# A gated graph network on one core: gates before the state update, row sums one chunk earlier, the residual kept in DRAM

## The reference, cut to what matters

```python
state = x
for _ in range(5):
    s_in, s_out = state @ in_W.T + in_b, state @ out_W.T + out_b
    a_in, a_out = A @ s_in, A.T @ s_out
    a = concat([a_in, a_out, state])
    r, z = sigmoid(a @ r_W.T + r_b), sigmoid(a @ z_W.T + z_b)
    joined = concat([a_in, a_out, r * state])
    h_hat = tanh(joined @ h_W.T + h_b)
    state = (1 - z) * state + z * h_hat
out = tanh(state @ o1_W.T + o1_b) @ o2_W.T + o2_b
return layernorm(x + out)
```

## Time and profile before

| | before |
|---|---|
| median of 3 runs | 700.49 us |
| profiled execution, its own time | 700.8 us |
| its span (first to last instruction) | 699.0 us |
| PE busy | 665.0 us, 2940 matmuls |
| DVE busy | 528.2 us |
| ACT busy | 348.8 us |
| POOL busy | 61.9 us |
| granted TensorE clock, mean | 0.986 |

### The profile page before, as it was taken

How to read it: one execution, slowest core, us unless ns; L and a number is a source line. 1 busy time by engine, 2 the same in 40 slices (tenths; PEclk the granted TensorE clock), 3 DMA queues, 4 the chain that set the end, 5 groups by cost and what they waited for, 6 DMA issues and landing times.

```text
span 699.0 us, 8537 instructions
## 1 busy us (share of the span) xinstructions
PE 665.0 (95%) x2940; PEld 539.7 (77%) x2940; DVE 528.2 (76%) x838; ACT 348.8 (50%) x486; POOL 61.9 (9%) x56
## 2 busy tenths in 40 slices
PE   8999999979999998999999989999998999999894
PEld 8888888757887886788778767877886788787783
DVE  4976776899577858867686797687768957856886
ACT  2955463646256236625452664356074715623555
POOL 0040204910000000000000000000000000004302
PEclk9999999989999999999999999999999999999998
DMA  9991621221000221200003021000312100013003
GB/s 294 379 371 45 229 67 49 42 61 30 3 0 31 57 35 43 35 13 0 30 33 57 15 46 30 0 30 30 51 40 60 30 1 1 8 61 120 1 1 123
DMA packets 91474, 44.62 MB, mean 64 GB/s; under 512 B 72112, under 2 KB 80944, under 8 KB 91184
## 3 DMA queue, kind: packets, MB, share of 16 engines
q1 hardware_dynamic: 87088, 43.67, 22.0%
q10 hardware_dynamic: 4352, 0.53, 0.5%
HBM read 32.12 MB, written 9.44 MB: 59 GB/s over the span
## 4 chain that ended last, share of the span: by engine, by line
PE 70%; DVE 16%; ACT 8%; issue 4%; ACTq 0%; POOL 0%; DVEq 0%; POOLq 0%
PE bank L546 25%; PE bank L597 12%; PE bank L533 10%; PE bank L535 10%; PE bank L534 10%; DVE work L1226 3%; ACT ring L792 2%; ACT ring L814 2%; DVE work L1245 2%; ACT work L885 2%; DVE work L1248 2%; DVE rows L1094 2%; PE bank L690 2%; DVE work L1232 1%; DVE stateT L1253 1%
## 5 line engine op out<-in xcount | busy, mean ns | idle before, releaser
L546 PE MATMUL bank<-ring,rows 128*128 128x512 f32 x768 | 178.6, 389 | 0.0
L885 ACT ACTIVATE work<-work,bias 128x512 f32<-128x512 f32 x120 | 85.8, 722 | 180.1 <-DVE work L1226 179.9
L546 PEld LDWEIGHTS bank<-ring,rows 128*128 128x128 f32 x768 | 144.1, 188 | 29.9
L1226 DVE SCALAR_TENSOR_TENSOR work<-degree,deg_w,bank 128x512 f32<-128x512 uint16 x120 | 88.6, 741 | 50.7 <-PE bank L535 50.4
L533 PE MATMUL bank<-u_c,fold 128*128 128x512 f32 x240 | 95.5, 398 | 7.7 <-DVE work L1226 7.7
L535 PE MATMUL bank<-u_c,fold 128*128 128x512 f32 x240 | 94.4, 393 | 0.0
L534 PE MATMUL bank<-u_c,fold 128*128 128x512 f32 x240 | 94.1, 392 | 0.0
L533 PE MATMUL bank<-st_c,own 128*128 128x512 f32 x160 | 63.9, 399 | 10.4 <-DVE work L1226 8.1
L597 PE MATMUL bank<-ring,rows 128*128 128x512 f32 x256 | 67.2, 394 | 0.3 <-DVE rows L1094 0.2
L534 PE MATMUL bank<-st_c,own 128*128 128x512 f32 x160 | 62.8, 393 | 0.0
L535 PE MATMUL bank<-st_c,own 128*128 128x512 f32 x160 | 62.8, 392 | 0.0
(11 more groups left out here) (148 smaller groups left out, 981.8 us busy)
## 6 DMA issues: line engine op xcount, KB each, us to landing
stage<-in_adj_dram SPq DMA_DIRECT2D x15, 512.0 KB, 7.0
sums<-in_adj_dram SPq DMA_DIRECT2D x13, 512.0 KB, 6.1
turned_dram<-work SPq DMA_DIRECT2D x12, 512.0 KB, 2.6
rows<-turned_dram SPq DMA_DIRECT2D x192, 32.0 KB, 2.0
work<-in_x_dram SPq DMA_DIRECT2D x4, 512.0 KB, 9.7
a<-in_x_dram SPq DMA_DIRECT2D x4, 512.0 KB, 5.3
a<-in_adj_dram SPq DMA_DIRECT2D x3, 512.0 KB, 10.1
rows<-work SPq DMA_DIRECT2D x48, 32.0 KB, 2.0
```

Source lines behind the costliest of these rows:

```text
L546: m = nc.tensor.matmul(u_bank[2 * (c % 2) + d][:, :], rows[:, part, j, d * P:(d + 1) * P], tile[:, jj, :], start=(first and jj == 0 and pa ...
L885: nc.scalar.activation(gates[:, g, e, :], gates[:, g, e, :], ACT.Tanh if g == H else ACT.Sigmoid, bias=bias[:, g, e:e + 1]).then_inc(gate_ ...
L1226: nc.vector.scalar_tensor_tensor(out=gates[:, g, e, :], in0=degree[:, c * CW:(c + 1) * CW], scalar=deg_w[:, g, e:e + 1], in1=g_bank[s % 3] ...
```

## The change

Arithmetic, matmuls and casts are the same; what differs is their order, two places of storage and one DMA round trip.

- DVE in chunk 1 (steps 1 to 4) and chunk 3: subtract, `gate` 0, multiply, add, `gate` 1, `rs` 0, then `turn_state`; a new wait of `rs` on the new state.
- T1 to T4 are formed in chunk 2, at (2, 2) and (2, 3), T1 and T2 also split there, before the split of chunk 3's state and U; the rest of the rows after `gate` 3 of chunk 3, in all steps.
- ACT casts the four ring tiles of the next side one at a time in chunks 1 and 3, between the gates. In `aggregate_pair` it does casts 5 to 9 in one piece, then, on side 0, one `row_high` of chunk 2's rows and two DMAs before cast 10 and the same before cast 11.
- C21 (`mix`) is kept in `gates[:, H, 0]` and no more in `temp[1]`.
- POOL does `sum_blocks(1)` after the last rows of step 1 are split. Step 0's rows DMAs (`turn_load(0, 0)` and `(0, 1)`) wait for 26 and 28 pairs used where they waited for 32.
- POOL adds o2_b to x in step 0, four operations, before the first `sum_bytes`; SP stores the sum to DRAM (`x_dram`) and loads it back at the end. The eight additions at the end are gone. DVE waits for the stores before it overwrites x.
- The degrees of chunk 3 are formed during chunk 2.

```diff
@@ sync @@
                 if t == 0:
-                    sp.wait_ge(pair_used, S_PAIR)
+                    sp.wait_ge(pair_used, (NC - 1) * NP + 2 * (k + 1))
...
+                        sp.dma_start(o2_bb, o2_b.partition_broadcast(P)).then_inc(o2_b_loaded, 16)
...
+                    if q == 2 * NP + len(AGAIN):
+                        for k in range(NC):
+                            sp.wait_ge(x_plus, k + 1)
+                            sp.dma_start(x_dram[:, k * BC:(k + 1) * BC, :], x_raw[:, k * BC:(k + 1) * BC, :]).then_inc(x_kept[k], 16)
...
-                sp.dma_start(x_res[c], x_v[:, c * BC:(c + 1) * BC, :]).then_inc(xr_loaded, 16)
+                sp.wait_ge(x_kept[c], 16)
+                sp.dma_start(x_res[c], x_dram[:, c * BC:(c + 1) * BC, :]).then_inc(xr_loaded, 16)
@@ gpsimd @@
+            pool.wait_ge(o2_b_loaded, 16)
+            pool.wait_ge(x_hi, NC)
+            pool.wait_ge(x_read, NC * DB)
+            pool.wait_ge(x_split, NC)
+            for c in range(NC):
+                xc = x_raw[:, c * BC:(c + 1) * BC, :]
+                nc.gpsimd.tensor_tensor(xc, xc, o2_bb[:, :].unsqueeze(1).broadcast_to([P, BC, D]), ALU.add).then_inc(x_plus, 1)
...
-            for side in range(2):
-                sum_blocks(side)
-
-            pool.wait_ge(o2_b_loaded, 16)
-            pool.wait_ge(xr_loaded, 16 * NC)
-            for b in range(NB // 2):
-                xr = x_res[b // 2][:, b % 2 * 2:b % 2 * 2 + 2, :]
-                nc.gpsimd.tensor_tensor(xr, xr, o2_bb[:, :].unsqueeze(1).broadcast_to([P, 2, D]), ALU.add)\
-                    .then_inc(residual_ready, 1)
+            sum_blocks(0)
+
+            pool.wait_ge(row_lo, row_count(1, (NC - 1, 1)))
+            sum_blocks(1)
@@ scalar @@
                 for s in range(GATE):
-                    if c == NC - 1 and not last:
-                        for op in (HIGH_FIRST if first else HIGH_LATER)[s]:
-                            row_high(t + 1, *op)
+                    if (c, s) == (NC - 2, 2 * DB - 1) and not last:
+                        row_high(t + 1, T1, 0)
+                        row_high(t + 1, T2, 0)
                     gate(t, c, s)
+                    if first and (c, s) == (NC - 2, 0):
+                        degree_part(NC - 1)
...
-                        if c == 0:
-                            for k in range(RING):
-                                cast(t, 1, k)
-                        elif not last:
-                            for k in range(RING):
-                                cast(t + 1, 0, k)
...
+            def gate_chunk_two(t, c, first, last):
...
+                high_rows(2)
+                if c == 1:
+                    next_cast()
+                gate(t, c, 0)
+                high_rows(3)
+                next_cast()
+                gate(t, c, 1)
+                rs_high(t, c, 0)
...
+                next_cast()
+                gate(t, c, 2)
...
+                    rs_high(t, c, 1)
+                next_cast()
+                gate(t, c, 3)
+                next_cast()
+                gate(t, c, 4)
+                gate(t, c, 5)
@@ scalar, aggregate_pair @@
                 cast(t, side, 4)
                 copy_p1(t, side)
-                for k in range(5, 8):
+                for k in range(5, 10):
                     cast(t, side, k)
-                if side == 0:
-                    for h in range(2):
-                        row_high(t, 2, h)
-                for k in range(8, 10):
-                    cast(t, side, k)
-                if side == 0:
-                    turn_move(t - 1)
                 for k in range(10, 12):
+                    if side == 0:
+                        row_high(t, 2, k - 10)
+                        turn_move(t - 1, range(2 * (k - 10), 2 * (k - 9)))
                     cast(t, side, k)
@@ vector @@
-                if t > 0 and s == GATE - 1 and c % 2 == 0:
+                if t == c == 0 and e == 0:
+                    dve.wait_ge(x_kept[g], 16)
+                if t > 0 and g == H and c % 2 == 0:
                     dve.wait_ge(u_lo, t * S_TWO + (c + 2) * TWO)
...
+                if t == c == e == 0:
+                    dve.wait_ge(x_kept[NG], 16)
+                if c == NC - 1 or c == 1 and t > 0:
+                    dve.wait_ge(state_new, t * S_TWO + (c - 1) * TWO + e + 1)
...
                     nc.vector.tensor_tensor(tmp[:, e, :], gates[:, H, e, :], old[e], ALU.subtract).then_inc(chain, 1)
+                if first_gate:
+                    first_gate()
...
+            ROWS_AT = {(2, 2): [("add", T1), ("add", T2)], (2, 3): [("low", ROWS[0]), ("low", ROWS[1]), ("add", T4), ("add", T3)],
+                       (3, 3): [("low", op) for op in ROWS[2:5]],
+                       (3, 4): [("low", ROWS[5])], (3, 5): [("low", ROWS[6])]}
...
-                    update(t, c - 1)
+                    update(t, c - 1, first_gate=lambda: gate(t, c, 0))
+                    next_pair(0)
+                    gate(t, c, 1)
+                    rs(t, c, 0)
+                    final(0)
                     if not last:
                         turn_state(t, c - 1)
-                gate(t, c, 0)
-                final(0)
-                next_pair(0)
...
                 gate(t, c, 3)
                 next_pair(3)
+                next_rows(3)
                 if c == NC - 2 or c == 0 and not first:
                     for e in range(DB):
                         split_state(t, c + 1, e)
...
-                next_rows(3)
```

More of the change, by code:

```diff
@@ L198, in fast_path @@
         scratch = ident[:, :].bitcast(U8)
-        o2_bb = flat_stage[:, 0:D].bitcast(F32)
+        o2_bb = late[:, 0:D]
         SQ, NQ = 32, P // 32
@@ L298, in fast_path @@
         xr_loaded = sem("f_xr_loaded")
-        residual_ready = sem("f_residual_ready")
+        x_plus = sem("f_x_plus")
+        x_kept = [sem(f"f_x_kept{c}") for c in range(NC)]
         stats_ready = sem("f_stats_ready")
@@ L626, in gate_chunk @@
                         count_odd()
+                    if first and (c, s) == (NC - 2, 2):
+                        pe.wait_ge(degree_read, c + 1)
+                        degrees(NC - 1)
                     if s == 0:
@@ L857, in turn_move @@
                 for n in range(NQ - 1, NQ):
-                    for r in range(NQ):
+                    for r in some:
                         act.dma_start(rows[n * SQ:(n + 1) * SQ, LO, k * BC:(k + 1) * BC, :].bitcast(F32)
@@ L898, in gate_chunk @@
                     act.wait_ge(b_loaded, 16 * (NG + 1))
+                if c == NC - 1 or c == 1 and not first:
+                    return gate_chunk_two(t, c, first, last)
                 for s in range(GATE):
-                    if c == NC - 1 and not last:
-                        for op in (HIGH_FIRST if first else HIGH_LATER)[s]:
-                            row_high(t + 1, *op)
+                    if (c, s) == (NC - 2, 2 * DB - 1) and not last:
+                        row_high(t + 1, T1, 0)
+                        row_high(t + 1, T2, 0)
                     gate(t, c, s)
+                    if first and (c, s) == (NC - 2, 0):
+                        degree_part(NC - 1)
                     if s < DB:
                         rs_high(t, c, s)
-                    if last and (c, s) == (NC - 1, DB - 1):
-                        hidden(1)
                     if last and (c, s) in FINAL_AT:
@@ L923, in gate_chunk, with high_rows, next_cast @@
                             split_u(t, c + 1, d, first)
-                        if c == 0:
-                            for k in range(RING):
-                                cast(t, 1, k)
-                        elif not last:
-                            for k in range(RING):
-                                cast(t + 1, 0, k)
                     if last and (c, s) == (NC - 2, GATE - 1):
                         hidden(0)
-                if c == NC - 2 and not first and not last:
-                    row_high(t + 1, T1, 0)
+            def gate_chunk_two(t, c, first, last):
+                ending = last and c == NC - 1
+                rows_ahead = iter(ROWS[2:7] if c == NC - 1 and not last else ())
+                casts = iter(() if ending else range(RING))
+                def high_rows(n):
+                    for _ in range(n):
+                        for op in rows_ahead:
+                            row_high(t + 1, *op)
+                            break
+                def next_cast():
+                    for k in casts:
+                        cast(*((t, 1) if c == 1 else (t + 1, 0)), k)
+                        break
+                high_rows(2)
[6 more added lines that the diff above has]
+                rs_high(t, c, 0)
+                if ending:
+                    rs_high(t, c, 1)
+                    hidden(1)
+                next_cast()
+                gate(t, c, 2)
+                if ending:
+                    final_split(FINAL_AT[c, 2])
+                else:
+                    rs_high(t, c, 1)
```

(14 more changed lines are left out.)

59 lines of the change are left out of this document (28 added, 31 removed).

## The result

The changed kernel takes 678.96 us (median of 4 runs, 678.11 to 679.61) against 700.67 us for the kernel before (4 runs, 698.12 to 701.02) on the same chip: ratio 0.9697, 95% interval 0.9671 to 0.9723. It is faster, by 21.7 us; 677 had been forecast, in a range of 671 to 687. The profiled execution took 679.28 us, of which the span is 677.5.

The account below looks back on a forecast made before the run. PE was busy 665.0 of 699.0 us, so only its idle time and time at the lower clock could be won. From 700.8 us, -15.0 - 4.0 - 3.7 + 1.6 - 2.8 = -23.9 gave 677 us, range 671 to 687.

Parts of the forecast that it names:

- the x stores: Step 0: storing x plus bias early was to cost nothing, or up to 1 us if the stores land late.
- Chunk 3, steps 1 to 3: Gate chunk 3: PE never waits, the chunk falls to 16.32 us from 21.84 or 20.26: -15.0 us.
- Chunk 1: Gate chunk 1, steps 1 to 4: falls from 17.47 to 16.32 us, half counted in step 4: -4.0 us.
- Chunk 3, step 0: Before chunk 3: wait of 2.7 us and one clock dip of 1.5, P1 at 153.1 instead of 156.84: -3.7 us.
- U of side 0: Side 0, steps 1 to 4: wait at P7 traded for a longer one at P5, 29.2 us: +1.6 us.
- The last step: With POOL's eight additions gone, hidden layer 0 and chunk 2 lose their delay: -2.8 us.
- 1: Waits move to r * state, 1 us in each of eight second chunks: 685, or 689 with dips; chance 0.15.
- 2: PE does not wait at P5, or less, and step 0 draws no clock dip: 670 us; chance 0.10.
- 3: The wait at P5 draws the clock down in two or three sides: 681 us; chance 0.10.
- 4: Slower: T2 on DVE waits for rows about 12 us later than in the trace: 704 us; chance 0.02.
- 5: Nothing is gained, because the granted clock or DVE's total (528.2 of 699) holds: 699 us; chance 0.03.

Follow-up runs that it names:

- rows_back: Changed kernel with T3, T4 and the first two low parts put back into chunk 3 on DVE in steps 1 to 3, ACT's high parts with them: 684.69 us.
- update_first: Changed kernel with DVE's update and turning again ahead of bank 0, and the first r * state ahead of bank 1; ACT's list as changed: 692.6 us.
- casts_back: Changed kernel with ACT's four ring casts put back together ahead of tanh, in chunks 0 and 2; DVE's new order stays: 683.96 us.
- p5_first: Changed kernel with DVE's two P5 casts moved ahead of the low part that waits for ACT: 671.46 us, ratio 0.959 to the kernel before.
- stores_order: Changed kernel with the four stores of x sent as quarters 0, 3, 1, 2: 678.3 us.
- residual_back: Changed kernel with x and the bias again added by POOL at the end, from the input, and nothing stored early: 681.69 us.
- rows_wait: Changed kernel with SP again waiting for all 32 pairs before it sends T2's rows in step 0: 683.71 us.
- both_back: Changed kernel with DVE's old update order and ACT's ring casts together ahead of tanh, but ACT's r * state splits as changed: 699.85 us, ratio 0.9992 to the kernel before.
- all_back: Changed kernel with DVE's old update order, ACT's r * state splits and the ring casts all put back; row sums stay in chunk 2: 690.86 us.
- update_act_first: Changed kernel with DVE's old update order and ACT's r * state splits back right behind their gates; ring casts stay spread: 694.3 us.

## Why the prediction was right, and where it was not

The sum came out 2.4 us too low against the profiled execution, 676.9 to 679.28: 1.1 are the x stores, the largest miss, 0.7 the sides, 0.5 the start. The mechanisms were the right ones.

- **Chunk 3, steps 1 to 3: forecast -15.0, measured -15.0.** All three at 16.32. rows_back, update_first and casts_back show that all three moves are needed: putting back one costs 1.8, 2.7 and 0.6 a chunk. The prediction laid out one list with all of them and did not price them apart; they don't add. My expectations for the old order missed by 4 and 8 us (684 to 689 against 692.6, and 692 against 699.85; the second was made by adding).
- **Chunk 1: forecast -4.0, measured -3.9** (1.15, 1.11, 1.12 and 0.53 in steps 1 to 4).
- **Chunk 3, step 0: forecast P1 at 153.1, measured 154.85.** Its own part is right: the wait was forecast as 2.7 and is 2.53 by the record (2.69 from start to start), and the dip came, which was luck in part: p5_first and rows_back have the same wait and no dip. P1 is 1.75 late because the chunks before it are: 1.1 from the stores and 0.5 from the start. The timeline of PE:

```profile
136.82 0.74 PE L543 MATMUL bank<-st_c,own 128*128 128x512 f32 x1 [2.53 <-DVE st_c L1131]
137.36 0.63 PE L544 MATMUL bank<-st_c,own 128*128 128x512 f32 x1
```

- **The term that was mis-sized most is the x stores**, "Cost nothing; if the stores land late, up to 1". They landed late, and chunk 0 of step 0 takes 17.42 in place of 16.32. Waits in the stretch from 20 to 75 us:

```profile
DVE work L1276 <- DMA x_dram<-work: 3.9, 1, 3.9
...
DVE work L1286 <- DMA x_dram<-work: 1.8, 1, 1.8
```

The page's part 6 (issues, KB each, us to landing):

```profile
x_dram<-work SPq DMA_DIRECT2D x4, 512.0 KB, 8.2
```

and the timeline of SP there:

```profile
48.00 3.95 SPq L423 DMA_DIRECT2D sums<-in_adj_dram  x3
52.01 3.57 SPq L412 DMA_DIRECT2D x_dram<-work  x4
```

The forecast took 2.6 us a store from the earlier trace rows, stores that had the queues to themselves, and let SP reach them at 48.9. SP reached them at 52.01, and each took 8.2 us behind the loads of the last pairs. The last landed by 62.89, when DVE's r * state stops waiting, not at 59.5. POOL's additions had no part in it: they ran from 36.59 to 46.08, within the 44 to 47 of the forecast. The bound of 1 us was right, nearly: it was 1.1. stores_order confirms the cause: quarter 3 ahead of 1 and 2 takes the 1.1 us away.
- **U of side 0: forecast +1.6 for four steps at 29.2, measured +2.3** (29.46, 29.49, 29.46, 29.37 against 29.19, 28.79, 28.80, 28.74). DVE waits for ACT's row split, does the low part, then the first P5 cast; PE waits behind them. The timelines of DVE and of PE in step 2:

```profile
286.33 0.69 DVE L1131 TENSOR_TENSOR rows<-rows 128x512 fp32r<-128x512 f32 x1 [2.10 <-ACT rows L806]
286.94 2.35 DVE L1140 TENSOR_TENSOR ring<-a 128x1024 fp32r<-128x1024 uint8 x2
```

```profile
288.29 2.27 PE L607 MATMUL bank<-ring,rows 128*128 128x512 f32 x8 [1.26 <-DVE ring L1140]
```

P5 starts 11.03 us after P1 (288.29 less 277.26), where 10.9 had been laid out; the side is 1.8 over side 1's 27.68, where 1.55 had been. p5_first takes all of it away.
- **The last step: forecast -2.8, measured -2.8** (chunk 2 0.6, hidden layer 0 2.1, the rest 0.1); residual_back brings the cost of POOL's additions back, 3.3 us, in part at other places.
- **Left over:** the first product of step 0 starts 0.5 us later (25.04 against 24.54), ahead of anything that the change touches. In the twelve kernels of the experiments the same start lies between 24.88 and 25.50, though no edit touches it, so it scatters by 0.6 us. Why all lie above the one execution of the kernel before is open.

Of the rivals, 1 did not come (no wait for a split of r * state in chunks 1 to 3; the margin was 0.8 us, so it was near). 2 is what p5_first makes of the kernel, 671.5 where 670 had been worked out. 3 did not come: the four waits of 1.3 us drew no dip. 4 needed rows that come late; rows_wait makes it in step 0 alone, and it costs 4.8 us. 5 fell with the time: neither the clock nor DVE's total held PE, since both second chunks run at 16.32.

## What to carry to other kernels

When the busiest engine waits in only some of its like stages, subtract the stage in which nothing waits (that difference was the gain of chunks 1 and 3 here, to 0.1 us), and lay the helper engines' lists out, in their order, against the times at which each result is wanted: the largest single find, 6.8 us by the windows and 7.5 by the medians, was two casts behind one low part that waited for another engine. Undoing one engine's order while another keeps the matching one measures a kernel that never was (both_back, 699.85, against all_back, 690.86), so put matching orders back together, and expect such parts not to add.

## What the runs showed of the hardware

- **DVE's byte casts are held by POOL.** No row of the kernel before showed it; in step 1 of the changed kernel the byte sums run beside three of them. Timelines of DVE and of POOL:

```profile
174.30 0.69 DVE L1142 CAST ring<-a 128x1024 fp32r<-128x1024 uint8 x1
175.44 1.24 DVE L1142 CAST ring<-a 128x1024 fp32r<-128x1024 uint8 x1 [0.46 <-PE bank L556]
177.26 0.87 DVE L1142 CAST ring<-a 128x1024 fp32r<-128x1024 uint8 x1 [0.57 <-PE bank L556]
```

```profile
174.46 1.67 POOL L505 TENSOR_TENSOR stage<-a 128x512 uint32<-128x512 uint32 x1 [41.38 <-DVE rows L1131]
176.21 1.37 POOL L505 TENSOR_TENSOR stage<-stage,byte_one 128x512 uint32<-128x512 uint32 x1
```

A cast that takes 0.69 took 1.24 and 0.87. Both ended 0.55 us after the POOL instruction that was running when they began (176.68 after 176.13, 178.13 after 177.58). The Trainium skill (SBUF — State Buffer, "Who interferes with whom") states that a DVE cast in a two-port mode takes the pair of ports that DVE shares with POOL, and that whichever engine issued first blocks the other until its instruction ends. The two ends agree with that. PE lost nothing by it: the side took 29.46.
- **The same idle stretch does or does not draw the clock down.** PE's wait of 2.53 us ahead of chunk 3 of step 0 was followed by the lower level in the changed kernel (clock 0.91 in the window, 0.63 us a record) and by the full one in p5_first and rows_back (1.00, 0.39). Of the ten kernels whose trace has this wait at 2.5 us, five show the dip right behind it (the changed kernel, casts_back, update_first, residual_back, stores_order). The wait of 1.99 us in update_act_first was followed by a dip three times in three, 1.9 us in the kernel before two times in three, and 1.72 us in update_first never in three. One dip is 1.3 to 1.6 us, the size of differences that one is tempted to explain.
- **The same three loads took SP 2.65 to 4.77 us to issue, and the cause is open.** They took 4.23 us from 37.17 in the changed kernel, 3.84 from 37.45 in stores_order and 4.77 from 37.31 in p5_first, in each beside POOL's additions to x, but 2.65 from 37.52 in residual_back, without them. POOL is not idle there either (its first byte sum, 2.42 us, runs from 37.53), and in the kernel before three loads from 44.66 took 4.24 us with POOL idle. So the additions go with the slow issue of this group, one execution of each, and are not shown to cause it.
